# Reordering the seam between the experts' layer and the second self-attention of a fused decoder

## The chip, the cores and the metric
The kernel runs on one core of a Trainium2 chip. The metric is the device time of one execution in microseconds. The core has TensorE (PE, matrix products; PEld is its loading of weights), VectorE (DVE), ScalarE (ACT), GpSimd (POOL) and SyncE (SP, which only issues transfers). Each engine works through its own list of instructions in order, and engines meet at semaphores.

## The reference
`x` is 8 sequences of 128 rows by 512 columns. Two decoder layers, each of self-attention, a second block and a feed-forward block, every one followed by `x = layernorm(x + block(x))`. Two blocks meet at the place of the change. Layer 0's feed-forward is a base matrix with low-rank experts:

```
base = xf @ base_W.T
top_vals, top_idx = top_k(xf @ gate_W.T, 2); top_probs = softmax(top_vals)
h = einsum('nd,erd->ner', xf, lora_A) * (gate_full * 2)[:, :, None]     # 28 experts, rank 8
out = base + einsum('ner,eor->no', h, lora_B)
```

Layer 1's self-attention (32 heads of 16) follows:

```
q, k, v = split(clip(x @ Wqkv.T, -8, 8)); q, k = layernorm(q)*w+b, layernorm(k)*w+b
scores = q k^T / 4 + slopes * (key - query), causal; out = softmax(scores) v; out @ Wout.T
```

## The kernel before
**Experts' layer.** The eight batches (sequences) go in four trips of two slots (`each` does both slots). A trip's steps are: `x_to_features` (PE turns x, ACT and DVE split it into a high and a low part; every fp32 product is made of three such, `mm3`), `gates_and_rank` (PE: logits and low-rank inputs), `top_gates` (DVE: two largest), `gate_exp` (ACT), `gated` (DVE: normed gates by rank inputs, L2313 to L2317), `base` (PE, 24 products of 512 columns), `gated_to_rank` (PE turns the gated values, L1055), `gated_split` (ACT L1550, DVE L2323), `experts_out` (PE), `close_layer` or `residual` (DVE L2219 to L2235 adds and takes moments, POOL `rstd` L1848, ACT `norm_x` L1340).

**Self-attention of layer 1** is a chain of `attention_step(1, i)`, i from FIRST = -8, four steps to a batch; each engine has a function of that name and does its part of step i. Before the scores of batch 0 (i = 0) the steps prepare: -8 turns x of batch 0; -6 and -5 project q and k of batch 0; -4 turns x of batch 1 and q of batch 0; -3 turns k of batch 0; -2 (START) and -1 project q and k of batch 1. Step 0 scores, turns x of batch 2 and q of batch 1; step 1 scores, projects v of batch 0, turns k of batch 1. A projected q or k (q0, k0, q1, k1 by batch) is clipped by DVE (L2116), gets moments (L2123 to L2125), a reciprocal root from POOL (`token_rstd`, L1802), and is normed by DVE (L2132). PE turns it (L839), ACT scales it into `qk` in eight operations (L1391), and for k SP then writes constant rows into `qk` with eight transfers (`extra_rows`, L681); a batch's scores (L880, masks L854) wait for these. DVE takes their maxima (`maxima`, L2142); scores of step i+1 wait for the maxima of step i. x of a batch is split by ACT (L1361) and DVE (`x_rows_rest`, L2065).

**The order** is written out by hand for each engine: the lists below interleave trips 2 and 3 of the experts' layer with steps FIRST to START. `due(i, kind)` says which batch's q or k is normed in step i: for i < 0 the one projected in that step, for i > 0 the one of the step before. DVE takes the moments and the norm at the end of a step for i < 0; for i > 0 the moments come after the maxima and the norm later in the step. POOL also splits weight pieces (L1881, L1883) between these steps, and sets ones for the values by four memsets (`ones_and_values`, L1781) once trip 3 is normed.

Of the kernel before, what the change touches and what calls it, by code (L numbers as in the profile page):

```python
# [17 lines left out]
TRIPS = B // SLOTS  # L18
# [8 lines left out]
FIRST, LAST = -2 * STEPS, STEPS * B + 11  # L27
# [82 lines left out]
def decoder(nc, a, out):  # L110
# [6 lines left out]
    A0, AC, MOE, A1, XA, FF = range(LAYERS)  # L117
    NORMED_BY_ACT = (MOE,)
    es = ExitStack()
    with es:  # L120
# [320 lines left out]
        def seq(trip, y, j=1):  # L441

            return nth(trip, 1, j, {A0: 0, MOE: 1, A1: 2, XA: 3}[y] * TRIPS)
# [47 lines left out]
        def of_step(i, kind):  # L491

            b = i // STEPS + M_BATCH[kind]
            return b if kind in kinds(i) and 0 <= b < B else None
# [16 lines left out]

        def due(i, kind):

            if i <= 0:
                return of_step(i, kind) if i < 0 else None
            return of_step(i - 1, kind)

        def scored(i):

# [234 lines left out]
        def _(pe):  # L754
# [166 lines left out]
            def attention_step(l, i):  # L921

                b, r = i // STEPS, i % STEPS
                if of_step(i, "max") is not None:
                    maxima_turned(l, b - 1)
                scores(l, i)
                if r == 1 and 0 <= b - 2 < B:
                    weigh_values(l, b - 2, 1)
                if r == 3 and 0 <= b - 1 < B:
                    weigh_values(l, b - 1, 0)  # L930
                if of_step(i, "x") is not None:
                    x_rows_turned(l, b + 2)
                if of_step(i, "o") is not None:
                    attention_out(l, b - 3)
                if of_step(i, "qT") is not None:
                    rows_turned(l, 0, b + 1)
                if of_step(i, "v") is not None:
                    projected(l, "v", b)
                if of_step(i, "kT") is not None:
                    rows_turned(l, 1, b + 1)  # L940
                for kind in "qk":
                    if of_step(i, kind) is not None:
                        projected(l, kind, b + 2)
# [239 lines left out]
            def each(step, trip, *args):  # L1183
                for s in both:
                    step(trip, s, *args)
# [64 lines left out]
            for i in range(FIRST + 3, FIRST + 5):  # L1250
                attention_step(1, i)
            each(gates_and_rank, 3)
            each(base, 3)
            attention_step(1, FIRST + 5)
            each(gated_to_rank, 3)
            each(experts_out, 3)
            for i in range(START, DRAIN):
                attention_step(1, i)
            maxima_turned(1, B - 1)
            scores(1, DRAIN)  # L1260
# [64 lines left out]
        def _(act):  # L1325
# [102 lines left out]
            def attention_step(l, i):  # L1428

                pieces, before = ((pieces_during_A0, 0), (pieces_during_A1, PIECES_A1))[l]  # L1430
                b, r = i // STEPS, i % STEPS
                if of_step(i, "max") is not None:
                    maxima_rows(l, b - 1)
                if of_step(i - 1, "kT") is not None:
                    qk_split(l, 1, b + 1)
                    if l == 0 and b + 1 == 0:
                        extra_rows_of_first()
                if scored(i - LAG):
                    probs(l, i - LAG)
                if of_step(i, "x") is not None and (l, b + 2) != (0, 0):  # L1440
                    x_rows_split(l, b + 2)
                if r == 3 and 0 <= b - 2 < B:
                    o_split(l, b - 2)
                if of_step(i, "qT") is not None:
                    qk_split(l, 0, b + 1)
                if l == 0 and i in W0_STEPS:
                    first_weights(2 + W0_STEPS.index(i))
                if r == 1 and 0 <= b < B:
                    split_hi(pieces(b // 2), b % 2, b // 2, 2, before)
# [188 lines left out]
            def each(step, trip, *args):  # L1638
                for s in both:
                    step(trip, s, *args)  # L1640
# [57 lines left out]
            close_layer(2)  # L1698
            each(gate_exp, 3)
            attention_step(1, FIRST + 5)  # L1700
            each(gated_split, 3)
            attention_step(1, FIRST + 6)
            close_layer(3)
            for i in range(START + 1, DRAIN + 1):
                attention_step(1, i)
# [54 lines left out]
        def _(pool):  # L1760
# [17 lines left out]
            def ones_and_values():  # L1778
                for i in range(2):
                    for e in range(2):  # L1780
                        nc.gpsimd.memset(ones_of(i, e), 1.0).then_inc(consts_ready, 1)  # L1781
# [36 lines left out]
            def attention_step(l, i):  # L1818

                pieces, done = ((pieces_during_A0, 0), (pieces_during_A1, PIECES_A0 + len(HALVED)))[l]  # L1820
                y = (A0, A1)[l]
                b, r = i // STEPS, i % STEPS
                if l == 1 and i == 0:
                    for s in both:
                        pool.wait_ge(x_ready[s], seq(TRIPS - 1, MOE))
                    ones_and_values()
                if l == 0 and i == 2 * STEPS:
                    pool.wait_ge(ld_c, 16 * EARLY)
                    qk_tables()
                if r == 3 and 0 <= b - 2 < B:  # L1830
                    o_rest(l, b - 2)
                if l == 1 and due(i, "q") is not None:
                    token_rstd(0, due(i, "q"))
                if l == 1 and due(i, "k") is not None:
                    token_rstd(1, due(i, "k"))
                if r == 2 and 0 <= b - 3 < B:
                    norm_rows(y, b - 3)
                if l == 0 and of_step(i, "x") is not None:
                    add_bias(b + 2)
                if r == 1 and 0 <= b < B:  # L1840
                    split_lo(pieces(b // 2), b % 2, b // 2, 2, done)
                if l == 1 and STEPS * B <= i < STEPS * B + KT:
                    pool.wait_ge(v_ready, batch(1, B - 1))
                    split(pieces_from_A1(), i - STEPS * B, 0, 0, PIECES_XV, PIECES_ALONE)
# [166 lines left out]
            for p in range(4 + 3 * KT, 6 + 3 * KT):  # L2011
                piece(p)
            each(rstd, MOE, 2)
            for i in range(FIRST + 3, FIRST + 6):
                attention_step(1, i)
            each(rstd, MOE, 3)
            for i in range(START, DRAIN + 4):
                attention_step(1, i)
            rest = pieces_from_A1()
            o_rest(1, B - 1)  # L2020
# [18 lines left out]
        def _(dve):  # L2039
# [145 lines left out]
            def attention_step(l, i):  # L2185

                b, r = i // STEPS, i % STEPS
                if of_step(i - 1, "v") is not None:
                    values(l, b)
                if of_step(i - 1, "o") is not None:  # L2190
                    add_branch(l, b - 3)
                if scored(i):
                    maxima(l, i)
                for n, kind in enumerate("qk"):
                    if l == 1 and i > 0 and due(i, kind) is not None:
                        token_moments(n, due(i, kind))
                if of_step(i, "x") is not None and (l, b + 2) != (0, 0):
                    x_rows_rest(l, b + 2)
                if of_step(i - 1, "o") is not None:
                    row_moments(l, b - 3)  # L2200
                if r == 1 and 0 <= b - 2 < B:
                    sums_turned(l, b - 2)
                if r == 2 and 0 <= b - 2 < B:
                    weighed(l, b - 2)
                for n, kind in enumerate("qk"):
                    if l == 1 and i > 0 and due(i, kind) is not None:
                        token_norm(n, due(i, kind))
                for n, kind in enumerate("qk"):
                    if of_step(i, kind) is not None:
                        (biased, clipped)[l](n, b + 2)  # L2210
                        if l == 1 and i < 0:
                            token_moments(n, b + 2)
                            token_norm(n, b + 2)
                if l == 0 and i in W0_STEPS:
                    first_weights(2 + W0_STEPS.index(i))
# [189 lines left out]
            def each(step, trip, *args):  # L2405
                for s in both:
                    step(trip, s, *args)
# [13 lines left out]
            def close_layer(trip):  # L2421
                each(residual, trip)
# [42 lines left out]
            attention_step(1, FIRST)  # L2465
            close_layer(1)
            each(top_gates, 2)
            for i in range(FIRST + 1, FIRST + 3):
                attention_step(1, i)
            each(gated, 2)  # L2470
            each(gated_split, 2)
            each(xT_split, 3, MOE, 0)
            close_layer(2)
# [3 lines left out]
            each(gated, 3)  # L2477
            attention_step(1, FIRST + 5)
            each(gated_split, 3)
            close_layer(3)  # L2480
            for i in range(START, DRAIN + 1):
                attention_step(1, i)
            xT_split(0, 0, XA, 2)
            dve.wait_ge(xT_hi[1], turned(0, XA))
# [112 lines left out]
```

## Time and profile before

| | us |
|---|---|
| median of 3 runs | 896.55 (896.06 to 898.69) |
| the profiled execution | 892.6 |
| its span | 890.8 |
| PE busy | 842.2 (95%) |
| DVE busy | 578.9 (65%) |
| ACT busy | 430.4 (48%) |
| POOL busy | 260.8 (29%) |
| mean granted clock of TensorE | 0.991 |

Times in the rows further down are us from the start of the span. The span is what the profiler records; the execution is 1.8 us longer. In the timeline a row is one instruction or some like ones in sequence, with its start, its length, its engine and line, what it writes and reads, and in brackets how long the engine sat idle before it and which engine's work ended that. "issue" there means that no engine's work shown ended it.

### The profile page before, as it was taken

The numbers are of one execution on the slowest core, as the hardware profiler recorded it, in microseconds if no ns is written. First come the engines' busy times: TensorE is split into PE (matmuls) and PEld (weight loads), VectorE is DVE, ScalarE is ACT, GpSimd is POOL, SyncE is SP. The second block draws the span as 40 slices with busy tenths as digits, with TensorE's granted clock in tenths as the row PEclk, the third lists the DMA queues.
The fourth block names the chain that finished last, engine by engine and source line by source line (L and its number), as shares of the span: only waits on it lengthen the run. The fifth ranks groups of instructions, "written<-read, shape, count | busy, mean of one in ns | idle before, by whom it ended". The sixth has DMA issues, their size and how long they took to land.

```text
span 890.8 us, 22438 instructions
## 1 busy us (share of the span) xinstructions
PE 842.2 (95%) x9192; PEld 683.8 (77%) x9192; DVE 578.9 (65%) x1519; ACT 430.4 (48%) x1101; POOL 260.8 (29%) x310
## 2 busy tenths in 40 slices
PE   6999999999999988999998999899999999999995
PEld 4777777675556766777776788799998899889983
DVE  3555666567786676567776644996476747665776
ACT  4254344458774333465555335443544365436532
POOL 1121332368986632002223338740000100010001
PEclk9999999999999999999999999999999999999998
DMA  7400000222220200000000102330000010000001
GB/s 230 159 26 15 21 14 23 62 71 66 70 78 29 72 19 7 17 18 18 19 20 21 37 19 80 100 103 25 1 1 2 2 48 1 2 1 24 2 1 48
DMA packets 20085, 35.05 MB, mean 39 GB/s; under 512 B 3120, under 2 KB 7344, under 8 KB 19728
## 3 DMA queue, kind: packets, MB, share of 16 engines
q1 hardware_dynamic: 19936, 33.56, 12.4%
q8 instruction: 73, 1.20, 0.5%
q14 instruction: 28, 0.23, 0.1%
q10 hardware_dynamic: 48, 0.07, 0.0%
HBM read 29.16 MB, written 2.10 MB: 35 GB/s over the span
## 4 chain that ended last, share of the span: by engine, by line
PE 78%; DVE 11%; ACT 3%; issue 3%; POOL 2%; DMA 1%; SPq 1%; POOLq 0%; DVEq 0%; ACTq 0%
PE bank L759 17%; PE bank L761 16%; PE bank L760 16%; PE bank L880 6%; PE bank L1151 4%; DVE tank L2357 3%; PE bank L901 3%; PE bank L1015 2%; PE bank L854 2%; PE bank L885 2%; PE bank L839 1%; DVE tank L2142 1%; PE bank L1002 1%; DVE tank L2367 1%; SPq L681 1%
## 5 line engine op out<-in xcount | busy, mean ns | idle before, releaser
L759 PE MATMUL bank<-wr,hTl 128*128 128x512 f32 (+3 forms) x472 | 188.9, 400 | 5.1 <-DVE wr L2071 2.6
L761 PE MATMUL bank<-wr,hTh 128*128 128x512 f32 (+3 forms) x472 | 180.6, 383 | 0.0
L760 PE MATMUL bank<-wr,hTh 128*128 128x512 f32 (+3 forms) x472 | 180.1, 382 | 0.0
L2142 DVE TENSOR_REDUCE tank<-bank 128x4 f32<-128x512 f32 x128 | 82.2, 684 | 51.9 <-PE bank L854 51.9
L759 PEld LDWEIGHTS bank<-wr,hTl 128*128 128x128 f32 (+1 forms) x472 | 89.3, 189 | 29.8 <-issue 9.3
L1419 ACT ACTIVATE pT<-bank 128x512 f32<-128x512 f32 x128 | 70.1, 606 | 82.3 <-PE bank L854 82.2
L761 PEld LDWEIGHTS bank<-wr,hTh 128*128 128x128 f32 (+1 forms) x472 | 89.3, 189 | 17.2
L760 PEld LDWEIGHTS bank<-wr,hTh 128*128 128x128 f32 (+1 forms) x472 | 89.6, 190 | 15.0 <-issue 1.0
L880 PE MATMUL bank<-qk 32*128 32x128 f32 x1024 | 76.0, 287 | 12.8 <-DVE tank L2142 4.8
L880 PEld LDWEIGHTS bank<-qk 32*128 32x128 f32 x1024 | 63.9, 190 | 30.1 <-issue 23.0
L885 PE MATMUL bank<-qk 32*128 32x128 f32 x1024 | 75.7, 287 | 0.3 <-DMA qk<-tank 0.3
L759 PE MATMUL bank<-hTh,wr 128*128 128x256 f32 (+1 forms) x240 | 73.3, 305 | 1.5 <-DVE hTl L2328 1.5
L761 PE MATMUL bank<-hTh,wr 128*128 128x256 f32 (+1 forms) x240 | 72.9, 304 | 0.0
L760 PE MATMUL bank<-hTl,wr 128*128 128x256 f32 (+1 forms) x240 | 72.8, 303 | 0.0
L1614 ACT ACTIVATE tank<-bank,stats 128x256 f32<-128x256 f32 x128 | 58.7, 482 | 23.8 <-DVE stats L2351 23.8
L885 PEld LDWEIGHTS bank<-qk 32*128 32x128 f32 x1024 | 63.3, 189 | 4.0 <-issue 3.0
L1391 ACT ACTIVATE qk<-bank,qk_shift,qk_scale 128x128 f32<-128x128 f32 x128 | 46.6, 478 | 21.8 <-PE bank L839 21.8
L2350 DVE TENSOR_REDUCE stats<-bank 128x2 f32<-128x512 f32 x64 | 43.8, 684 | 18.8 <-PE bank L761 18.8
L1859 POOL TENSOR_TENSOR stats<-stats,half 128x1 f32<-128x1 f32 x7 | 3.8, 549 | 174.8 <-DVE stats L2403 174.8
L1622 ACT CAST hTh<-bank 128x384 fp32r<-128x384 f32 x32 | 15.3, 479 | 81.3 <-PE bank L1151 81.3
L2357 DVE COPY tank<-bank 128x512 f32<-128x512 f32 x64 | 39.7, 682 | 22.0 <-PE bank L1135 22.0
L1874 POOL TENSOR_TENSOR wr<-raw,wr 128x512 fp32r<-128x512 f32 (+3 forms) x23 | 25.0, 1090 | 82.0 <-ACT wr L1352 82.0
(242 smaller groups left out, 1849.3 us busy)
## 6 DMA issues: line engine op xcount, KB each, us to landing
raw<-w_qkv_dram SPq DMA_DIRECT2D x12, 256.0 KB, 2.9
raw<-w_xq_dram SPq DMA_DIRECT2D x16, 192.0 KB, 2.4
raw<-w_xo_dram SPq DMA_DIRECT2D x12, 256.0 KB, 2.8
x_all<-x_dram SPq DMA_DIRECT2D x8, 256.0 KB, 6.6
cin<-ctx_dram SPq DMA_DIRECT2D x8, 256.0 KB, 3.0
cin<-ctxT_dram SPq DMA_DIRECT2D x8, 256.0 KB, 2.8
out_dram<-x_all SPq DMA_DIRECT2D x8, 256.0 KB, 2.0
qk<-extra_dram SPq DMA_DIRECT2D x124, 16.0 KB
```

The source lines that it names most:

```text
L759: mm(dst, lhs[1], rhs[0], start=start, stop=False)
L760: mm(dst, lhs[0], rhs[1], start=False, stop=False)
L761: return mm(dst, lhs[0], rhs[0], start=False, stop=stop)
L880: ins = mm(s_bank[n][:, at], qk[b % RING][g, e, m, :], qk[b % RING][g, 2 + e, m, :], start=m == 0, stop=True, skip_group_check=True)
L885: ins = mm(t_bank[n][:, at], qk[c % RING][g, 2 + f, m, :], qk[c % RING][g, f, m, :], start=m == 0, stop=True, skip_group_check=True)
L1151: ins = mm(bank[s][0][row:row + NARROW, tile * P:(tile + 1) * P], xv[s][:, at:at + NARROW], xpT[s][:, (2 * j + t) * P:(2 * j + t + 1) * P] ...
L1391: ins = av(qk[b % RING][:, 2 * i + e, m, :], m_bank[u % 2][:, m * P:(m + 1) * P], ACT.Identity, bias=qk_shift[:, i, e, m:m + 1], scale=qk_ ...
L1419: av(pT[e][:, 2 * rows + n, :], t_bank[n][:, :], ACT.Exp).then_inc(exp_ready, 1)
L1614: ins = av(xp[s][:, h * XT:(h + 1) * XT], bank[s][i][:, j * XT:(j + 1) * XT], ACT.Exp, bias=st[s][:, NEGMAX.start + h:NEGMAX.start + h + 1 ...
L2142: v.tensor_reduce(nm[b % 2][:, at:at + KT], s_bank[n][:, :].rearrange("p (m t) -> p m t", m=KT), AX, ALU.max, negate=True).then_inc(max_re ...
L2350: steps_done(XA, trip, v.tensor_reduce(r, bank[s][i][:, :].rearrange("p (h t) -> p h t", h=2), AX, ALU.max))
L2357: v.tensor_copy(xpT[s][:, i * 512:(i + 1) * 512], bank[s][i][:, :]).then_inc(xpT_ready[s], 1)
```

## The change
PE turns k of batch 0 (step -3) ahead of base of trip 3, and projects q of batch 1 (START) between `gated_to_rank` and `experts_out` of trip 3. ACT splits that k ahead of `gated_split` of trip 3. DVE does `gated` of trip 2 ahead of the steps that hold q of batch 0, and q of batch 1 ahead of trip 3's residuals. `due` gives k of batch 1 to step 0, so DVE takes its moments behind the first maxima; POOL does q of batch 1 ahead of trip 3's `rstd`, and k of batch 1 in step 0, ahead of the memsets.

```
         def due(i, kind):
-            if i <= 0:
-                return of_step(i, kind) if i < 0 else None
-            return of_step(i - 1, kind)
+            if i < -1:
+                return of_step(i, kind)
+            return of_step(i - 1, kind) if i >= 0 else None
...  PE
             each(gates_and_rank, 3)
+            attention_step(1, FIRST + 5)
             each(base, 3)
-            attention_step(1, FIRST + 5)
             each(gated_to_rank, 3)
+            attention_step(1, START)
             each(experts_out, 3)
-            for i in range(START, DRAIN):
+            for i in range(START + 1, DRAIN):
...  ACT
             attention_step(1, FIRST + 5)
+            attention_step(1, START)
             each(gated_split, 3)
-            attention_step(1, FIRST + 6)
             close_layer(3)
...  POOL, attention_step
-                if l == 1 and i == 0:
-                    for s in both:
-                        pool.wait_ge(x_ready[s], seq(TRIPS - 1, MOE))
-                    ones_and_values()
...
                 if l == 1 and due(i, "k") is not None:
                     token_rstd(1, due(i, "k"))
+                if l == 1 and i == 0:
+                    for s in both:
+                        pool.wait_ge(x_ready[s], seq(TRIPS - 1, MOE))
+                    ones_and_values()
...  POOL, order
-            for i in range(FIRST + 3, FIRST + 6):
+            for i in range(FIRST + 3, START + 1):
                 attention_step(1, i)
             each(rstd, MOE, 3)
-            for i in range(START, DRAIN + 4):
+            for i in range(START + 1, DRAIN + 4):
...  DVE, attention_step (token_moments and token_norm)
-                    if l == 1 and i > 0 and due(i, kind) is not None:
+                    if l == 1 and i >= 0 and due(i, kind) is not None:
...
-                        if l == 1 and i < 0:
+                        if l == 1 and i < -1:
...  DVE, order
             each(top_gates, 2)
+            each(gated, 2)
             for i in range(FIRST + 1, FIRST + 3):
                 attention_step(1, i)
-            each(gated, 2)
...
             each(gated_split, 3)
+            attention_step(1, START)
             close_layer(3)
-            for i in range(START, DRAIN + 1):
+            for i in range(START + 1, DRAIN + 1):
```

## Rows read from the trace of the kernel before

**Rows 1.** The page's first part: engine, busy us, share of the span, instructions.
```profile
PE 842.2 (95%) x9192; PEld 683.8 (77%) x9192; DVE 578.9 (65%) x1519; ACT 430.4 (48%) x1101; POOL 260.8 (29%) x310
```

**Rows 2.** PE's timeline, 311 to 353: start, us, line, op, tiles, [idle before <-releaser].
```profile
311.38 0.39 PE L759 MATMUL bank<-wr,hTl 128*128 128x512 f32 x1
...
318.68 0.43 PE L1055 MATMUL bank<-ident,tank 128*112 128x128 f32 x2 [1.55 <-DVE tank L2317]
...
320.50 0.43 PE L1055 MATMUL bank<-ident,tank 128*112 128x128 f32 x2 [1.40 <-DVE tank L2317]
...
321.57 0.47 PE L759 MATMUL bank<-wr,hTl 112*128 112x512 f32 x1
...
328.23 0.63 PE L839 MATMUL bank<-ident,tank 128*128 128x128 f32 x4 [0.44 <-DVE tank L2116]
...
338.83 0.50 PE L759 MATMUL bank<-wr,hTl 112*128 112x512 f32 x1 [0.70 <-DVE hTl L2323]
...
348.58 1.16 PE L880 MATMUL bank<-qk 32*128 32x128 f32 x16 [1.24 <-issue]
...
349.89 0.66 PE L816 MATMUL bank<-ident,x_all 128*128 128x128 f32 x4
...
352.34 1.50 PE L880 MATMUL bank<-qk 32*128 32x128 f32 x16 [1.35 <-DVE tank L2142]
```

**Rows 3.** DVE's timeline, the gates of trips 2 and 3.
```profile
313.15 0.69 DVE L2116 TENSOR_SCALAR tank<-bank 128x512 f32<-128x512 f32 x1
...
316.39 1.26 DVE L2313 SCALAR_TENSOR_TENSOR gates<-gates 128x28 f32<-128x28 f32 x1
...
333.51 0.19 DVE L2313 SCALAR_TENSOR_TENSOR gates<-gates 128x28 f32<-128x28 f32 x1 [0.31 <-ACT gates L1545]
...
335.21 0.39 DVE L2317 TENSOR_TENSOR tank<-bank,gates 128x224 f32<-128x224 f32 x1
...
338.35 0.76 DVE L2323 TENSOR_TENSOR hTl<-bank,hTh 112x256 fp32r<-112x256 f32 x2 [2.75 <-ACT hTh L1550]
```

**Rows 4.** POOL's timeline: a weight piece's subtraction, the memsets.
```profile
316.27 1.34 POOL L1883 TENSOR_TENSOR wr<-raw,wr 128x512 fp32r<-128x512 f32 x1
...
350.00 1.34 POOL L1781 MEMSET tank<- 128x256 f32 x4
```

**Rows 5.** ACT's timeline: gate_exp 3, split of k of batch 0.
```profile
333.06 0.55 ACT L1545 ACTIVATE gates<-gates,stats 128x28 f32<-128x28 f32 x2
...
338.48 2.92 ACT L1391 ACTIVATE qk<-bank,qk_shift,qk_scale 128x128 f32<-128x128 f32 x8
```

**Rows 6.** SyncE, line 681, 341 to 348: xcount, ns min/median/max, first and last start.
```profile
L681 SPq DMA_DIRECT2D qk<-extra_dram x8: 612/620/737, 341.4 to 346.2; - x8
```

**Rows 7.** DVE's timeline, residuals of trip 3 to the second step of batch 0.
```profile
340.53 0.69 DVE L2219 TENSOR_TENSOR x_all<-bank,x_all 128x512 f32<-128x512 f32 x1 [1.43 <-PE bank L761]
...
344.66 0.69 DVE L2116 TENSOR_SCALAR tank<-bank 128x512 f32<-128x512 f32 x1 [0.43 <-PE bank L761]
...
347.62 0.68 DVE L2116 TENSOR_SCALAR tank<-bank 128x512 f32<-128x512 f32 x1
...
350.09 1.00 DVE L2132 TENSOR_SCALAR tank<-tank,stats 128x512 f32<-128x512 f32 x1 [0.66 <-POOL stats L1802]
...
351.01 1.27 DVE L2142 TENSOR_REDUCE tank<-bank 128x4 f32<-128x512 f32 x2
...
352.21 0.67 DVE L2065 TENSOR_TENSOR hTl<-bank,hTh 128x512 fp32r<-128x512 f32 x1
```

**Rows 8.** PE in a window (busy, granted clock, DMA share, GB/s); its timeline.
```profile
353.00:354.00 1.00, 1.00 (x18) 0.50 0.00 0
...
358.04 0.60 PE L839 MATMUL bank<-ident,tank 128*128 128x128 f32 x4
```

**Rows 9.** PE's timeline, the start of batch 1's scores.
```profile
368.56 1.16 PE L880 MATMUL bank<-qk 32*128 32x128 f32 x16 [1.21 <-issue]
```

**Rows 10.** PE's waits, 400 to 540: waited for, us in total, times, longest.
```profile
PE bank L880 <- DMA qk<-extra_dram: 2.5, 1, 2.5
```

More of the change, by code:

```diff
@@ L2205, in attention_step @@
                 for n, kind in enumerate("qk"):
-                    if l == 1 and i > 0 and due(i, kind) is not None:
+                    if l == 1 and i >= 0 and due(i, kind) is not None:
                         token_norm(n, due(i, kind))
```

## The prediction

> **What bounds the kernel now.** I read the page first: TensorE (PE) is busy 95% of the span and no other engine comes near [rows 1], so only PE's idle time, or PE time at a lowered clock, can be won. Next I read PE's timeline over the stretch that the diff touches, from base of trip 2 to the second step of scores of layer 1. Six waits stand there [rows 2]: 1.55 and 1.40 us ahead of gated_to_rank 2, 0.44 ahead of qT of batch 0, 0.70 ahead of experts_out 3, 1.24 ahead of scores(0), 1.35 ahead of scores(1). With the one further on at 368.56 [rows 9] that is 7.9 us; the six are 6.7. Then I asked, in the timelines of VectorE (DVE), GpSimd (POOL), ScalarE (ACT) and SyncE, what ends each of the waits.
>
> **Gates of trip 2 ahead of q of batch 0 on DVE.** Base 2 begins at 311.38 and PE is through with it at 318.68 - 1.55 = 317.13. DVE begins q's clipping at 313.15 and the gates' first operation only at 316.39, and that operation takes 1.26 us; in trip 3 the same one takes 0.19 [rows 3]. POOL's subtraction on a weight piece runs from 316.27 to 317.61 [rows 4], and the DVE operation ends 0.04 after it: it was held up. The second slot's is held up alike: both slots take from 316.39 to the second transposition at 320.50, 4.1 us; in trip 3 from 333.51 to 335.60, 2.1 us. After the change gated begins at about 313.2, when POOL has nothing to run (its pieces stand behind q's rstd in its queue), and ends at 315.3. Both PE waits go: 2.95 us.
> What comes late instead: q's chain, which stood between 313.15 and 316.39 (3.2 us), now runs 315.3 to 318.5, then DVE's gated_split 2 of one slot (0.4, half of the row of 338.35) to 318.9, and PE sees it at 319.0. PE is there by 317.13 + 0.23 (first transposition) + 1.07 (320.50 to 321.57, second transposition and x_to_features) = 318.4, so a new wait of 0.6 remains. Experts_out 2 starts at 319.0 instead of 321.57: **2.6 us**. POOL's pieces follow q's rstd about 2.1 us later; the DVE work that they then lie over reads one operand from PSUM.
> The Trainium skill, page "SBUF — State Buffer", section "Who interferes with whom", says that a VectorE operation with two SBUF inputs and a GpSimd one that reads SBUF exclude each other for the whole instruction. The gates' operation has two SBUF inputs, and 1.26 against 0.19 agrees. Without that rule, were the 1.26 its own length, gated would end near 317.3 and experts_out 2 about 1.9 later than I say: the part would be worth 0.7.
>
> **q of batch 1 between gated_to_rank 3 and experts_out 3.** The 0.70 wait is for DVE's part of the split of hT. Experts_out 3 and the projections of q1 and k1 fill 338.83 to 347.34 (348.58 - 1.24) [rows 2], about 2.8 each; one projection now lies in between: **0.7 us**. The 0.44 stays.
>
> **k of batch 0 turned and split sooner.** scores(0) waits for no engine; it waits for the constant rows of qk[0]. ACT splits k0 at 338.48 for 2.9 us [rows 5], then SP issues eight transfers, 341.4 to 346.9 (346.2 + 0.62) [rows 6], and the scores start 1.7 after. After the change PE turns k0 behind gates 3, ahead of base 3. ACT is free of gate_exp at 333.6 [rows 5] - 2.6 = 331.0, splits to 333.9, SP ends at 339.4, landed at 341.1. PE comes there at 347.34 - 2.6 - 0.7 = 344.0. The **1.24 us** go with 2.9 to spare; at its old place in ACT's queue k0's rows would land at 348.58 - 2.6 = 346.0 and the wait be 2.0, which is what this step is worth to PE once the others are made. SP's queue holds nothing else meanwhile.
>
> **DVE between q1 and scores(1).** scores(1) waits 1.35 us for maxima(0), which DVE begins at 351.01 because k1's norm stands ahead (350.09, 1.00 us, over POOL's four memsets [rows 4]) [rows 7]. The change puts the maxima first. But now q1's chain stands ahead of trip 3's residuals. Step by step: PE ends gated_to_rank 3 at 338.83 - 0.70 = 338.13, less 2.6, and q1 2.8 later, at 338.3. DVE: q1 2.96 (344.66 to 347.62) to 341.3, both residuals 3.7 (340.53 to 344.66 less 0.43 idle) to 345.0, k1 clipped 0.7 to 345.7, maxima(0) 1.27 to 346.95. PE: scores(0) 344.0 to 345.35, x2 and a short wait, q1 turned at 345.7 to 346.2, scores(1) at 347.0 instead of 352.34. So **5.3 us are won by then**, of which 2.6 + 0.7 + 1.24 are above and 0.8 are this wait; 0.7 of waiting stays, and DVE sets it.
> Next late: DVE does k1's moments (1.1: 347.62 to 350.09, less 0.68 for the clipping and 0.66 idle) and then x2's low half (0.67, row of 352.21) by 348.7; scores(1) ends at 348.3 and v(0) waits for that half, **0.4 us lost**. k1's rstd precedes the memsets in POOL now, and its norm, 0.55 alone to 1.00 over the memsets, ends by 349.7; k1 is turned at 351.5, so 1.8 cover it. ACT's x2 and q1 splits come behind trip 3's norm (about 346.9) and end near 350.3, 1.2 ahead of their use.
>
> **The clock.** At 353 PE's granted clock is 0.50, 1.2 instead of 2.4 GHz [rows 8], behind the 1.24 and 1.35 of idleness. scores(1) to k1's turning take 352.34 to 358.04, 5.7 us, where 1.3 (a step of scores, 348.58 to 349.89) and 2.8 make 4.1 to 4.2: 1.5 lost, so some 3 us were spent at the lower level. About 1.1 us of idleness are left here of 2.6, in smaller pieces, and two waits of 1.55 and 1.40 around 318 lowered nothing in this execution (experts_out 2 behind them begins with a matmul of 0.47 us, experts_out 3 with one of 0.50 [rows 2]). Bounds: **1.5 won** if the clock stays up, 0 if it falls as before. I take the first, being nearer to the stretch at 318 in idleness. The Trainium skill, "TensorE: Matmul & The Clock Gate", section "What's actually happening", says that the activity window runs freely and isn't aligned with the kernel, so that the same program can meet it at another phase; no row here shows a second execution. By it a fall may appear or stay away by chance.
>
> **Sum.** 2.6 + 0.7 + 1.24 + 0.8 - 0.4 + 1.5 = 6.4 us, and 4.9 without the clock. From batch 1's scores on, nothing in the order of work is changed. The wait at 368.56 is for the constant rows of batch 1: 10.5 us from k1's turning at 358.04, with 9.3 of PE work between, both shifted alike [rows 8, 9]; it stays with its 1.2. The longest later one in this layer, 2.5 us on batch 7's constant rows [rows 10], hangs on the same chain of splits, and shifts too. The profiled execution took 892.6 with a span of 890.8; I expect 886.2 and 884.4. The median is 4 us above that execution; the same gain taken off 896.55 gives **890.2**.
>
> **Rivals.**
> (a) *The clock falls anyway* behind the small waits: all else as said, gain 4.9, 891.6. For it: scores fill 32 rows at a time, and the fall at 353 came in that work. Against: less idleness. 0.25.
> (b) *DVE is the new wait.* It has no pause from 338.3 to 349.3 but POOL's 0.7 in q1's chain. If the residuals or q1's chain are stretched (1.0 instead of 0.55 is seen), or POOL's pieces, now 2.1 us later, hold up a DVE operation as they did the gates' (1.1 each), scores(1) and x2's half are late by as much; 2 to 3 us of it leaves 893 to 894. 0.12.
> (c) *It does nothing*: the shift is absorbed by a later fixed arrival, such as weights. Each later load waits for a split, and the splits for steps, and up to 540 PE waits for nothing of POOL's, the longest wait being that of [rows 10]; 896.5. 0.08.
> (d) *Slower*: one mechanism, the lower clock. Earlier scores run in many light matmuls with 0.4 to 0.6 us holes; if the clock stays at 1.2 GHz over them, each us there costs 0.5. To turn 4.9 won into 2.7 lost takes 15 us of it, where 3 are seen; 20 us would give 901. 0.04.
>
> **How the numbers follow.** Forecast 0.51, the likeliest, 889 to 891.3 by itself. A measurement of this kernel can tell about 0.3%, 2.7 us. Forecast and (a), with most of (b), are faster: 0.85; (c) and the rest of (b) the same: 0.11; slower 0.04. The range is 887.5 (1.5 for one more fall of the clock avoided, and 1.2 of spread, half of what lies between the runs shown) to 894.0 (b).
>
> **What would show it.** Right: the first gates operation of trip 2 near 0.2 us; no wait ahead of either transposition of gated, one of 0.6 ahead of experts_out 2; SP's first constant rows near 334; scores(0) with no wait, at 344; scores(1) at 347 behind DVE's maxima; v(0) held briefly by x2's low half; k1 turned at 351.5 to 353; the wait before step 4 unchanged at 1.2. Wrong: step 4 of the scores not 5 us earlier than 368.56; or it is, and the end isn't.

## The result and the profile after

The changed kernel takes 886.57 us (median of 4 executions, 885.86 to 887.17) against 896.3 before (the median of 896.55 with one execution more): ratio 0.9882, 95% interval 0.9861 to 0.9904. That is 9.7 us where 6.4 were forecast, and below the stated range. The direction and the steps on the waits hold; the size doesn't. The two profiled executions alone tell another story: spans of 890.8 and 884.1, 6.7 us apart, with 884.4 forecast.

From the page of the changed kernel:

```profile
span 884.1 us, 22438 instructions
## 1 busy us (share of the span) xinstructions
PE 839.0 (95%) x9192; PEld 681.0 (77%) x9192; DVE 578.3 (65%) x1519; ACT 430.5 (49%) x1101; POOL 260.4 (29%) x310
```

PE's timeline of the changed kernel, from the transpositions of gated_to_rank 2 to batch 1's scores, answers to [rows 2, 8, 9]:

```profile
316.87 0.60 PE L1055 MATMUL bank<-ident,tank 128*112 128x128 f32 x4
...
318.77 0.50 PE L759 MATMUL bank<-wr,hTl 112*128 112x512 f32 x1 [0.43 <-DVE hTl L2324]
...
325.45 0.63 PE L839 MATMUL bank<-ident,tank 128*128 128x128 f32 x4 [0.44 <-DVE tank L2117]
...
337.97 0.39 PE L759 MATMUL bank<-wr,hTl 112*128 112x512 f32 x1
...
343.59 1.16 PE L880 MATMUL bank<-qk 32*128 32x128 f32 x16
...
346.68 1.16 PE L880 MATMUL bank<-qk 32*128 32x128 f32 x16 [0.48 <-DVE tank L2143]
...
348.37 0.47 PE L759 MATMUL bank<-wr 128*128 128x512 f32 x1 [0.31 <-DVE hTl L2066]
...
351.18 0.60 PE L839 MATMUL bank<-ident,tank 128*128 128x128 f32 x4
...
361.61 0.60 PE L880 MATMUL bank<-qk 32*128 32x128 f32 x6 [1.12 <-issue]
```

Both slots are turned with no wait; experts_out 3 (337.97) and scores(0) (343.59) have none. What is left are the small waits foretold: 0.43 for DVE's split, 0.44, 0.48 for the maxima, 0.31 for x2's low half, 1.7 in sum for the 6.7 of before. So the waits alone give 5.0. The wait at 361.61, ahead of scores(4), is the old one of 368.56.

DVE's timeline of the changed kernel, against [rows 3, 7]:

```profile
313.07 0.19 DVE L2314 SCALAR_TENSOR_TENSOR gates<-gates 128x28 f32<-128x28 f32 x1
...
338.17 0.69 DVE L2117 TENSOR_SCALAR tank<-bank 128x512 f32<-128x512 f32 x1 [1.83 <-PE bank L761]
...
341.12 0.68 DVE L2220 TENSOR_TENSOR x_all<-bank,x_all 128x512 f32<-128x512 f32 x1
...
345.34 1.28 DVE L2143 TENSOR_REDUCE tank<-bank 128x4 f32<-128x512 f32 x2
...
347.54 0.68 DVE L2066 TENSOR_TENSOR hTl<-bank,hTh 128x512 fp32r<-128x512 f32 x1
348.30 1.26 DVE L2133 TENSOR_SCALAR tank<-tank,stats 128x512 f32<-128x512 f32 x1
```

The gates' first operation takes 0.19 instead of 1.26. The maxima come straight behind k1's clipping; k1's norm still lies over POOL's memsets and takes 1.26. And ACT's and SP's, against [rows 5, 6]:

```profile
330.71 2.92 ACT L1392 ACTIVATE qk<-bank,qk_shift,qk_scale 128x128 f32<-128x128 f32 x8
```

```profile
333.66 26.32 SPq L681 DMA_DIRECT2D qk<-extra_dram  x16
```

PE in windows of 1 us in the changed kernel, against [rows 8]. Behind a window stand its length, PE's busy time and matmuls, the granted clock, the DMA share and GB/s:

```profile
347.00:348.00 1.00, 1.00 (x24) 1.00 0.00 0
363.00:364.00 1.00, 1.00 (x8) 1.00 0.63 184
364.00:365.00 1.00, 0.63 (x21) 1.00 0.04 12
481.00:482.00 1.00, 0.72 (x21) 0.92 0.11 21
```

A fall, below, is a stretch in which the granted clock is 0.50, 1.2 in place of 2.4 GHz. The changed kernel has none before 481, where one follows a wait of 2.5 us. The kernel before has two up to there. The prediction counts the one that begins at 353. The other begins at 370, behind the wait of 1.21 us ahead of scores(4); it also lasts 3.4 us, and the prediction leaves it out. Its windows:

```profile
370.00:371.00 1.00, 1.00 (x6) 0.54 0.57 195
373.00:374.00 1.00, 1.00 (x33) 0.76 0.00 0
```

PE's timeline around it, first of the kernel before, then of the changed one:

```profile
369.87 0.96 PE L816 MATMUL bank<-ident,x_all 128*128 128x128 f32 x4
...
373.92 0.50 PE L759 MATMUL bank<-wr 128*128 128x512 f32 x1
```

```profile
362.92 0.66 PE L816 MATMUL bank<-ident,x_all 128*128 128x128 f32 x4
...
366.08 0.47 PE L759 MATMUL bank<-wr 128*128 128x512 f32 x1 [0.19 <-DVE hTl L2066]
```

The same work takes 4.05 us with that fall and 3.16 without, so 0.9 are won there. At this place the changed kernel is 7.8 us ahead (373.92 and 366.08), at the end 6.7. The 1.1 between are given back behind 570, 0.6 of it by a wait for DVE ahead of L1151 that the kernel before doesn't have.

### The profile page after: what moved, and what is told of

Read it like the earlier page. It is cut to its first block, busy times and chain, and to the rows that moved or that the text cites. A ratio compares the mean times of both kernels' runs of the same rounds, so it can differ in the third digit from the quotient of the medians.

```text
span 884.1 us, 22438 instructions
## 1 busy us (share of the span) xinstructions
PE 839.0 (95%) x9192; PEld 681.0 (77%) x9192; DVE 578.3 (65%) x1519; ACT 430.5 (49%) x1101; POOL 260.4 (29%) x310
## 4 chain that ended last, share of the span: by engine, by line
PE 76%; DVE 13%; ACT 3%; issue 3%; POOL 2%; DMA 1%; SPq 1%; POOLq 0%; DVEq 0%; ACTq 0%
PE bank L759 17%; PE bank L761 15%; PE bank L760 15%; PE bank L880 6%; PE bank L1151 4%; DVE tank L2358 3%; PE bank L901 3%; PE bank L1015 2%; PE bank L854 2%; DVE tank L2368 2%; PE bank L885 2%; DVE tank L2143 1%; PE bank L839 1%; PE bank L1002 1%; SPq L681 1%
## 5 line engine op out<-in xcount | busy, mean ns | idle before, releaser
L880 PE MATMUL bank<-qk 32*128 32x128 f32 x1024 | 74.7, 284 | 11.1 <-DVE tank L2143 4.4
L880 PEld LDWEIGHTS bank<-qk 32*128 32x128 f32 x1024 | 62.7, 187 | 28.2 <-issue 21.6
L885 PE MATMUL bank<-qk 32*128 32x128 f32 x1024 | 74.7, 284 | 0.3 <-DMA qk<-tank 0.3
L885 PEld LDWEIGHTS bank<-qk 32*128 32x128 f32 x1024 | 62.4, 187 | 4.0 <-issue 3.0
L2368 DVE TENSOR_SCALAR tank<-tank,stats 128x256 f32<-128x256 f32 x128 | 47.5, 413 | 2.3
```

What stands on the lines that cost most here:

```text
L880: ins = mm(s_bank[n][:, at], qk[b % RING][g, e, m, :], qk[b % RING][g, 2 + e, m, :], start=m == 0, stop=True, skip_group_check=True)
L885: ins = mm(t_bank[n][:, at], qk[c % RING][g, 2 + f, m, :], qk[c % RING][g, f, m, :], start=m == 0, stop=True, skip_group_check=True)
L2368: ins = v.tensor_scalar(block, block, sums[:, j:j + 1], None, ALU.mult)
```

## The experiments

The question was where 3.3 us beyond the forecast came from. Theory 1: the clock falls behind waits in some executions and for varying lengths, the execution profiled before was one with few and short falls, and the change takes the causes away. Theory 2: that execution was off for a reason outside the stretch. Medians below are device times; spans are about 1.8 less.

**Both kernels again, and the change cut in two.** a_gates_only has DVE's `each(gated, 2)` ahead of steps FIRST + 1 and FIRST + 2 and nothing else; a_all_but_gates has all the rest.

```
             each(top_gates, 2)
+            each(gated, 2)
             for i in range(FIRST + 1, FIRST + 3):
                 attention_step(1, i)
-            each(gated, 2)
```

> The kernel before, unchanged, for a second trace. Theory 1 (clock): its executions differ among themselves by falls of the granted clock behind its waits (near 318, 352 and 368), each worth about 1.5 us, so spans run from 890 to 896 in such steps and a higher span goes with a lower mean clock. Theory 2 (luck of one execution): the profiled 892.6 was off for a reason outside the stretch of the change, such as loads at the start; then all spans here are near 894.5 with the clock at 0.991 or so, and the trace has its surplus before 300 us or behind 400.

> The changed kernel, unchanged. Both theories: 886 to 887 in the median, spans 884 to 885.5. Ratio to before 0.988 to 0.990; if the first comparison was the odd one, 0.993 (6.4 us).

> Only DVE's gates of trip 2 are moved ahead of q of batch 0. By the sum of the prediction 2.6 us; with theory 1 the waits of 2.95 us near 318 also cost falls of the clock in part of the executions, so 3.5 to 5 us in the median. Theory 2: 2.6 (0.997).

> The change without the move of the gates of trip 2. By the sum 3.8 us (0.7 + 1.24 + 0.8 - 0.4 + 1.5). Theory 1: together with the run that has the gates alone it gives the 9.7 to 10 of the whole, with 5 to 6 here. Theory 2: 3.8, and the two together make 6.4, with the rest unexplained.

| | median us | ratio to before, 95% | executions, spans |
|---|---|---|---|
| before_again | 896.88 | 1.0002 (0.9983 to 1.0022) | 12, 890.6 to 897.7 |
| after_again | 886.53 | 0.9884 (0.9863 to 0.9905) | 5, 883.7 to 885.5 |
| a_gates_only | 889.78 | 0.9927 (0.9905 to 0.9948) | 6, 886.3 to 891.6 |
| a_all_but_gates | 891.19 | 0.9938 (0.9920 to 0.9955) | 6, 888.5 to 890.7 |

The result repeats. The kernel before spreads over 7 us, the changed one over 2. Spans of the kernel before go with the mean clock: over 102 of its executions, taken from four sets of comparisons, the 10 with a mean clock of 0.984 average 897.4, the 23 with 0.990 average 892.9, the 4 with 0.991 average 890.8; the median span is 894.7. The profiled one of before (890.8, 0.991) would be the fourth shortest among them. Theory 1 has its first support; theory 2 asked for the same clock throughout. The second trace of the kernel before shows a fall of twice the length at the same place; PE in windows of 1 us:

```profile
351.00:352.00 1.00, 0.09 (x2) 1.00 0.00 0
352.00:353.00 1.00, 1.00 (x11) 0.55 0.00 0
...
358.00:359.00 1.00, 1.00 (x4) 0.54 0.00 0
359.00:360.00 1.00, 1.00 (x10) 1.00 0.00 0
```

It lasts from 352.1 to 358.9, 6.8 us, where the first trace had 3.4. The two parts win 6.8 and 5.4 us by medians, 12.2 together for 10. A second set of the first part, further down, makes that 10.4, so this alone doesn't show that they overlap.

**Filling the waits.** The kernel before with matmuls added in four waits, into a PSUM bank that nothing reads then; they compute nothing that is used. The order of work is untouched.

```
+            def filling(n, into):
+                for _ in range(n):
+                    mm(into, w_qkv1[0][:, 0, 0:P], w_qkv1[0][:, 0, 0:D], start=True, stop=True, skip_group_check=True)
...  ahead of gated_to_rank(2, s): 6 and 5; at the head of scores(1, 0) and scores(1, 1): 5 each
```

> The kernel before, with added matmuls (512 columns, into a PSUM bank that nothing reads then) in four of its waits: 6 and 5 ahead of the two transpositions of gated_to_rank 2, 5 ahead of scores(0), 5 ahead of scores(1). The waits keep their length, only PE is busy in them. Theory 1 (the clock falls behind these waits, differently from one execution to the next, and that makes the gap between 6.4 and 10 us): median 891 to 892.5, spread of the spans under 3 us in place of 7. If the rest of the gap has another cause: 896 to 897, as the kernel before.

Measured: 892.22, ratio 0.9951 (0.9933 to 0.9969), spans of 6 executions 888.6 to 891.9. Added work made the kernel 3.2 to 4.4 us faster: 3.2 against the kernel before of the same set (895.46), 4.4 by the ratio, and 4.3 by the median spans if all 102 executions are taken (894.7 and 890.4). The spread of the spans, 3.3, is a little over the 3 expected. PE's idle time ahead of scores(1) is now short and the clock stays up, as its timeline and a window show:

```profile
352.27 1.16 PE L889 MATMUL bank<-qk 32*128 32x128 f32 x16 [0.49 <-DVE tank L2153]
```

```profile
354.00:355.00 1.00, 1.00 (x6) 1.00 0.00 0
```

The order of work is the same and no wait is taken away, so what is won is clock: the falls that these waits bring cost the kernel before 3.2 to 4.4 us in the median, where the sum took in 1.5. They aren't all gone: this trace still has a fall of 6.8 us at 486, where the two of the kernel before have one of 3.4 and one of 6.8 near 489.

**Leaving one part out.** Each is the changed kernel with one part at its old place.

> The changed kernel with k of batch 0 turned and split at its old place. Constant rows land 2.0 to 2.4 us after PE is ready for scores(0). By the sum 888.5 to 889; with falls of the clock behind that wait 889.5 to 890.5. If the wait for the constant rows was a misreading: 886.5.

> The changed kernel with q of batch 1 projected behind experts_out 3, as before. The wait of 0.7 us ahead of experts_out 3 is back; q1's chain on DVE lies behind the residuals. By the sum 887.2, nothing from the clock.

> The changed kernel with the moments and norm of k of batch 1 ahead of the first maxima, as before. DVE gives maxima(0) 2.4 us later: a wait near 2.9 us ahead of scores(1). v(0) then doesn't wait. By the sum 888.5; with the clock falling behind the 2.9 us in most executions 890.

| | median us | over the changed kernel (886.53) | wait that returns | spans |
|---|---|---|---|---|
| no_k0_sooner | 892.73 | 6.2 | 2.10, scores(0) | 887.2 to 894.4 |
| no_q1_sooner | 887.95 | 1.4 | 0.70, experts_out 3 | 884.8 to 889.7 |
| no_k1_later | 892.02 | 5.5 | 3.53, scores(1) | 887.5 to 894.1 |

PE's timelines, of the first and of the third:

```profile
346.92 1.16 PE L880 MATMUL bank<-qk 32*128 32x128 f32 x16 [2.10 <-issue]
```

```profile
350.76 2.08 PE L880 MATMUL bank<-qk 32*128 32x128 f32 x16 [3.53 <-DVE tank L2143]
```

The first wait is the 2.0 of the prediction; it costs 6.2. One wait left is enough to bring the spread of 7 us back. In the third, sixteen scores' matmuls take 2.08 instead of 1.16 behind the wait. q1's place costs 1.4 for a wait of 0.7. By the ratios, each against the kernel before of its own set, the three cost 6.8, 2.2 and 6.5. The first and the third cost 2 us more than was expected even with falls (889.5 to 890.5, and 890), and the third wait was expected at 2.9. With a_all_but_gates (4.7 over the changed kernel) the four parts cost 17.8 when each is left out alone, for the 10 that all win together: their gains don't add up.

**Which waits.** Filling one pair at a time; no_k1_later filled with 12; and the changed kernel filled where it still waits (4 ahead of scores(4), 10 ahead of scores of step 28).

> The kernel before, with the added matmuls only in the two waits ahead of gated_to_rank 2. Moving the gates alone won 6.7 us where its waits are 2.5; if the other 4.2 are clock, by falls that begin with those two waits, this gives 892 to 893. If the falls begin with the waits near 348 and 352 whatever lies ahead of them (as in both traces of the kernel before), 895 to 896.

> The kernel before, with the added matmuls only ahead of scores(0) and scores(1). If falls begin with the waits near 348 and 352: 892 to 893, and no fall at 352 in its trace. If they begin with those ahead of gated_to_rank 2: 895.

> The changed kernel with the norm of k of batch 1 ahead of the first maxima as before, and 12 matmuls added in the wait of 3.5 us ahead of scores(1). The wait itself costs 3.0 of the 5.5 us that this order lost. If the other 2.5 are the clock: 889.5, with a spread of the spans under 3 us in place of 6.6. If they are something else of the order: 892.

> The changed kernel with 4 matmuls added ahead of scores(4) (wait 1.1 us) and 10 ahead of the scores of step 28 (wait 2.5 us, behind which the clock falls for about 4 us in every trace so far). If the fall is caused by that wait, it goes: 884.5 to 885. If it comes from what lies around it (light matmuls): 886.5, as without them.

| | median us | ratio to before, 95% |
|---|---|---|
| before_fill_gates_only | 896.37 | 0.9992 (0.9975 to 1.0008) |
| before_fill_scores_only | 893.74 | 0.9973 (0.9960 to 0.9986) |
| no_k1_filled | 890.74 | 0.9939 (0.9922 to 0.9956) |
| after_filled | 885.94 | 0.9889 (0.9868 to 0.9910) |

Filling ahead of gated_to_rank 2 alone does nothing, since the fall behind the scores' waits comes all the same; its windows:

```profile
352.00:353.00 1.00, 0.47 (x6) 0.88 0.00 0
359.00:360.00 1.00, 1.00 (x5) 0.71 0.00 0
```

Filling the waits ahead of the scores wins 2.5 to 2.8, filling all four 3.2 to 4.4, which the intervals don't separate. no_k1_filled came 1.3 below the unfilled one, not the 2.5 expected; its trace has a fall of 3.4 us at 368, which neither trace of the changed kernel has. In after_filled the fall at 481 is gone. First PE's timeline of the changed kernel at that place, then the filled one's with a window:

```profile
481.28 0.38 PE L880 MATMUL bank<-qk 32*128 32x128 f32 x2 [2.54 <-DMA qk<-extra_dram]
```

```profile
481.30 0.38 PE L889 MATMUL bank<-qk 32*128 32x128 f32 x2 [0.18 <-issue]
```

```profile
481.00:482.00 1.00, 0.82 (x25) 1.00 0.11 17
```

That fits a fall brought by that wait, but one trace doesn't show it: in a_all_but_gates PE waits 2.64 us at the same place, up to 487.07, and the clock stays up behind it, against what was expected of "every trace so far":

```profile
488.00:489.00 1.00, 1.00 (x29) 1.00 0.45 163
```

Over six executions the median of after_filled is 0.6 below the changed kernel and its ratio to before no better (0.9889 and 0.9884), so a gain isn't shown; three spans are 881.9 to 883.0, the others 885.2 to 886.4.

**What the gates' part alone wins.** a_gates_only was 6.8 us below the kernel before, with waits worth 2.6, though filling them gave nothing. Again the same kernel; with the scores' waits filled; and with 11 matmuls (2.6 us) ahead of the first attention step, so that the stretch stands later in time, in three orders of work:

```
             pe.wait_ge(w_split, FREE + PIECES_QKV1)
+            filling(11, bank[1][2][:, :])
             attention_step(1, FIRST)
```

> Once more only the gates of trip 2 moved. If the first set was luck: median 892 to 894, spans up to 893. If not: 889.8 again.

> The gates of trip 2 moved and 5 matmuls added ahead of each of scores(0) and scores(1). With both kinds of wait taken care of: 892.2 (the kernel before with all filled) less 0 to 0.6, plus what moving wins over filling, 2.6: 889.3 to 889.6. The difference to the unfilled one is what falls still cost there.

> The gates of trip 2 moved, and 11 matmuls (2.6 us) added ahead of the first attention step of layer 1, so that the stretch stands where it stood before in time. If the place in time decides whether the clock falls: 896 (the falls are back). If not: 889.8 + 2.6 = 892.4 (or 2.6 above what gates_alone_again gives).

> The kernel before with the same 11 matmuls. Without any effect of the place in time: 896.3 + 2.6 = 898.9. If the place decides: a median off that by 1.5 us or more, either way.

> The changed kernel with the same 11 matmuls (2.6 us) ahead of the first attention step of layer 1. If the surplus is falls of the clock behind the waits ahead of the scores: 886.5 + 2.6 = 889.1, and no fall near 350 in the trace. If it belongs to the matmuls themselves: 890.3.

| | median us | ratio to before, 95% | executions, spans |
|---|---|---|---|
| gates_alone_again | 891.44 | 0.9943 (0.9922 to 0.9963) | 10, 887.1 to 893.6 |
| gates_filled | 889.15 | 0.9915 (0.9890 to 0.9940) | 6, 887.0 to 888.9 |
| gates_shifted | 894.91 | 0.9977 (0.9961 to 0.9993) | 12, 890.6 to 895.6 |
| before_shifted | 900.09 | 1.0041 (1.0022 to 1.0060) | 12, 895.6 to 901.1 |
| after_shifted | 891.84 | 0.9925 (0.9896 to 0.9954) | 6, 884.4 to 892.3 |

Part was luck: the second set is 1.7 higher. Over both sets (16 executions) the median span is 889.15, 5.5 below before: 2.6 by waits, 2.9 by something else. Filling the scores' waits wins 1.8 in this kernel (889.15 and 887.35) and 2.8 in the kernel before (894.7 and 891.9), so about 1.0 of the 2.9 are falls at the scores that come less often once the gates are moved. The 2.6 us of added work cost 3.5 to 3.6 in two orders and 5.3 in the changed kernel, which I expected to take 2.6 (3.7 by the ratios). The intervals reach down to 2.6 or below in each, and before_shifted is 1.2 off its 898.9 where 1.5 was to count as an effect, so by the times alone an effect of the place isn't shown. The trace of after_shifted has no fall near 350, as expected, but one at 368, behind the 1.1 us wait ahead of scores(4), where the two traces of the changed kernel itself have none; that of before_shifted has one at 323, right behind the waits of gated_to_rank 2, and one of 10.2 us from 353.9:

```profile
368.00:369.00 1.00, 0.82 (x9) 0.58 0.40 146
374.00:375.00 1.00, 1.00 (x4) 0.51 0.00 0
```

```profile
323.00:324.00 1.00, 1.00 (x6) 0.58 0.66 187
353.00:354.00 1.00, 1.00 (x24) 0.94 0.05 16
363.00:364.00 1.00, 1.00 (x4) 0.50 0.00 0
364.00:365.00 1.00, 1.00 (x10) 0.94 0.00 0
```

**What the mean clocks say.** The span times what its mean clock lacks to 1 is an estimate of the time lost to the lower level. It is an upper one: it counts the end of the span, where PE is idle (2.7 us before, 3.1 after, in the profiled executions), and all of a fall: for the one at 370 it counts 1.7, and 0.9 were lost. Over the 102 executions of the kernel before, the spans have a standard deviation of 1.8 us, the spans times their mean clock one of 0.9.

| | executions | mean span, us | mean clock | lost, at most, us |
|---|---|---|---|---|
| before | 102 | 894.6 | 0.9879 | 10.9 |
| changed kernel | 9 | 884.8 | 0.9936 | 5.7 |
| before_filled | 6 | 890.4 | 0.9930 | 6.2 |
| before_fill_gates_only | 12 | 894.1 | 0.9880 | 10.7 |
| before_fill_scores_only | 12 | 892.1 | 0.9910 | 8.0 |
| gates alone, both sets | 16 | 889.3 | 0.9904 | 8.5 |
| no_k0_sooner | 12 | 890.6 | 0.9867 | 11.9 |
| no_k1_later | 12 | 890.7 | 0.9885 | 10.2 |
| no_k1_filled | 6 | 889.2 | 0.9912 | 7.9 |
| before_shifted | 12 | 898.6 | 0.9847 | 13.8 |
| after_shifted | 6 | 889.3 | 0.9903 | 8.6 |

The changed kernel is 9.8 us shorter and loses 5.2 less to the clock, which leaves 4.6 for the 5.0 of waits. before_filled is 4.2 shorter and loses 4.6 less: nothing else is needed. The gates alone are 5.2 shorter and lose 2.4 less, which leaves 2.9 for their 2.6 of waits. no_k1_filled is 4.4 longer than the changed kernel, and the clock has 2.2 of that. In no_k0_sooner the loss grows by 6.2, as much as that order costs in all although it waits 2.1 us too, so the estimate is too high there. Both shifted kernels in the table lose 2.9 more than unshifted, a sign that the place or the added work itself matters. Some traces have falls outside the stretch too (near 30 in six of the 19, near 560 in two), so not all of the loss is the seam's.

Whether a given wait brings a fall thus changes with execution and place. What decides it stays open.

## Why the prediction was wrong, step by step

Right, with forecast and trace:

- Gates of trip 2: the operation at 0.2 (0.19), no wait ahead of either transposition, experts_out 2 at 319.0 with 0.6 of waiting (318.77, 0.43). The operation took 1.26 beside POOL's subtraction and 0.19 without. The Trainium skill, page "SBUF — State Buffer", section "Who interferes with whom", says that a VectorE instruction with two SBUF inputs contends with a GpSimd one that reads SBUF; the two lengths agree. The alternative, 1.26 as the operation's own length, would have won 0.7 here, and 2.8 were won.
- k of batch 0: ACT's split at 331.0 (330.71), SP's first row at 333.9 (333.66), scores(0) at 344.0 without a wait (343.59). The 2.0 of waiting at its old place were met by 2.10 in no_k0_sooner.
- q of batch 1: the 0.70 gone; alone 1.4 by medians where 0.7 was forecast, with spans that spread over 5 us.
- DVE from q1 to the scores: q1 at 338.3 (338.17), maxima(0) from 345.7 (345.34), scores(1) at 347.0 (346.68), v(0) late by 0.4 (0.31), k1 turned at 351.5 (351.18). Only k1's norm over the memsets was longer, 1.26 for at most 1.00; its cover of 1.8 took it.
- The wait ahead of scores(4) stays: 1.2 (1.12). Batch 1's scores start 7.0 sooner; 6.4 were forecast.
- The execution profiled: 886.2 and span 884.4 (885.86 and 884.1). That is in part luck: the fall at 370, not in the sum, gave 0.9 more, and the work behind 570 took 1.1 back.

Wrong is the clock's term of the sum, **1.5 won**, with 0 to 1.5 as its bounds, and with it the step from the trace to the median, "the same gain taken off 896.55". The term was sized from the fall at 353 alone. That fall is gone and was worth its 1.5: scores(1) to k1's turning took 5.7 us and now take 4.5, 0.3 of them a new wait. But the trace of before has a second one in the stretch, at 370, behind the wait of 1.21 us that the sum leaves as it is; it was put at nothing without a reason, and went too.

More came by the median. The median of before was 4 us above its own profiled execution, and I let that stand as a constant that both kernels share. It was no constant: the changed kernel's median is 0.7 above its profiled execution. Waits give 5.0 of the 9.7 us, and the clock about 4.7 where 1.5 were forecast: filling the same four waits in the kernel before wins 3.2 to 4.4, and by the mean clocks the change loses at most 5.2 less. The low end, 887.5, allowed for one fall more and 1.2 of spread.

The Trainium skill's page "TensorE: Matmul & The Clock Gate", section "What's actually happening", says that the window over which activity is watched runs freely and doesn't restart with the kernel; the prediction concluded from it that a fall may appear or stay away by chance. 102 spans from 890.5 to 898.5, which go with their mean clocks, agree with that conclusion. I drew from it only that my gain was uncertain, and not that the profiled execution, at the fast end of the ones shown, had been spared.

Of the rivals, (a) would have left a fall near 353, and neither of the changed kernel's two traces has one; (b) saw DVE as the bound, which behind scores(0) it is, for 0.8 us in all; (c) and (d) didn't come. The rival missing was that the change takes away more of the low clock than one trace shows.

## What to carry to other kernels

Compare the profiled execution with the median before summing: a gap of 4 us beside a sum of 6 is a term of its own, and where the spans go with their mean clocks it is clock, which here hung on the waits. Then look for every fall in the trace, not just the first. A PE wait of 1 to 3 us among light matmuls cost here up to three times its length (6.2 for 2.1), and the parts of a change that each remove one don't add up (17.8 for 10), since one wait left can bring the falls back. Matmuls with unused results, put in such a wait, are a test for it that leaves the order of work alone.

## What the runs showed of the hardware

- Behind waits of 1.1 to 3.5 us PE's granted clock went from 2.4 to 1.2 GHz for 3.4 to 10.2 us (353.0 to 356.4 and 370.1 to 373.5 in the first trace, 352.1 to 358.9 in before_again, 353.9 to 364.1 in before_shifted), in part of the executions only: the waits of 1.55 and 1.40 us near 318 brought none in the first trace and one at 323 in before_shifted, and a wait of 2.64 us up to 487 brought none in a_all_but_gates.
- A fall of 3.4 us cost 1.5 us at 353 and 0.9 at 370.
- Added matmuls that keep PE busy in its waits made a kernel faster by 3.2 to 4.4 us of 896 (0.9951, 0.9933 to 0.9969).
- DVE's norm of 128 x 512 takes 0.55 us alone and 1.26 when POOL's four memsets start 0.09 ahead of it (348.21 and 348.30 in the changed kernel), though it took 1.00 in the first trace, where they start as near.
